# Moving expert weight splits between stages, and one subtraction between engines, in a four-layer kernel on one core

## Time and profile before

| | |
|---|---|
| median of three runs | 1728.53 us |
| profiled execution: time / span of the core | 1729.09 us / 1727.3 us |
| TensorE busy | 1576.4 us (91%) |
| VectorE busy | 1172.6 us (68%) |
| ScalarE busy | 931.7 us (54%) |
| GpSimd busy | 578.2 us (33%) |
| ternary layer | from about 652 to 907 us |
| features of the linear attention | from about 907 to 1094 us |
| its output and the routing | from about 1094 to 1206 us |

### The profile page before, as it was taken

One profiled execution on the slowest core, in us unless ns is written; L12 is line 12 of the kernel. 1 busy time (PEld: TensorE's weight loads), 2 busy tenths in 40 slices (PEclk: granted clock), 3 DMA queues, 4 the chain that ended last, 5 costly groups with the idle time before them and its releaser, 6 DMA issues. The chain is left out here.

```text
span 1727.3 us, 33567 instructions
## 1 busy us (share of the span) xinstructions
PE 1576.4 (91%) x12554; PEld 799.2 (46%) x12554; DVE 1172.6 (68%) x2074; ACT 931.7 (54%) x1641; POOL 578.2 (33%) x583
## 2 busy tenths in 40 slices
PE   5899999889999997999987999787898899999997
PEld 3533333354333343444433444454555566666564
DVE  4599998568999965899866777795623243333387
ACT  4756777445677765777645565476222333333332
POOL 4556565262000021222222121596271111111265
PEclk9999999999999999999998999899999999999999
DMA  6422331000000003666547999551151764456344
GB/s 232 140 55 56 69 75 38 13 2 2 14 2 2 2 2 77 137 143 137 105 91 267 320 330 336 198 180 68 63 94 50 279 234 167 154 186 220 99 125 135
DMA packets 177841, 211.42 MB, mean 122 GB/s; under 512 B 114202, under 2 KB 117624, under 8 KB 175504
## 3 DMA queue, kind: packets, MB, share of 16 engines
q1 hardware_dynamic: 170336, 188.54, 36.3%
q0 software_dynamic: 7344, 20.73, 4.5%
HBM read 193.33 MB, written 56.40 MB: 145 GB/s over the span
## 5 line engine op out<-in xcount | busy, mean ns | idle before, releaser
L751 ACT ACTIVATE layer_scratch<-banks 128x512 f32<-128x512 f32 x576 | 312.5, 595 | 129.5 <-PE banks L631 127.9
L862 DVE TENSOR_REDUCE layer_mx<-banks 128x2 f32<-128x1024 f32 (+3 forms) x304 | 339.2, 1155 | 24.1 <-PE banks L609 20.8
L2314 PE MATMUL banks<-wgate,sparse_xT 128*128 128x352 f16 x1128 | 184.4, 313 | 1.6 <-DVE sparse_xT L2392 1.6
L646 PE MATMUL banks<-layer_scratch,V 128*32 128x256 f32 x2304 | 174.5, 389 | 0.8 <-ACT layer_scratch L759 0.8
L2314 PEld LDWEIGHTS banks<-wgate,sparse_xT 128*128 128x128 f16 x1128 | 108.4, 98 | 62.1 <-DVE sparse_xT L2392 2.0
L1401 PE MATMUL banks<-arena,early 128*128 128x512 f16 x576 | 134.6, 384 | 0.3 <-DVE lin_relu L1561 0.3
L2398 DVE SCALAR_TENSOR_TENSOR sparse_hid<-sparse_th,banks 128x352 f32<-128x352 f32 x47 | 24.5, 521 | 154.0 <-ACT sparse_th L2359 154.0
L2425 POOL DMA_INDIRECT xg<-x_d,token x45 | 42.6, 947 | 249.2 <-PE banks L2304 249.2
L1840 PE MATMUL banks<-arena,xT 128*128 128x352 f16 x768 | 121.8, 315 | 2.0 <-PEq L2262 1.4
L1017 PE MATMUL banks<-wfcT,early 128*128 128x512 f16 x512 | 115.3, 383 | 7.3 <-ACT ffn_h L1159 6.5
L1145 PE MATMUL banks<-wprojT,ffn_hT 128*128 128x512 f16 x512 | 114.8, 383 | 7.3 <-DMA ffn_hT<-ffn_h 7.1
(11 more groups left out here) (300 smaller groups left out, 3033.4 us busy)
## 6 DMA issues: line engine op xcount, KB each, us to landing
wgate<-gate_d SPq DMA_DIRECT2D x47, 1408.0 KB
wdown<-down_d SPq DMA_DIRECT2D x47, 768.0 KB
lin_sp_raw<-in_L_ffn_w_gate_up_dram SPq DMA_DIRECT2D x52, 352.0 KB, 5.2
gate_d<-lin_sp_parts SPq DMA_DIRECT2D x52, 352.0 KB, 4.6
y_d<-y SPq DMA_DIRECT2D x47, 256.0 KB
down_d<-lin_sp_parts SPq DMA_DIRECT2D x39, 256.0 KB, 5.3
lin_sp_raw<-in_L_ffn_w_down_dram SPq DMA_DIRECT2D x26, 256.0 KB, 5.1
wfcT<-in_L_ffn_w_fc_dram SPq DMA_DIRECT2D x8, 512.0 KB, 8.2
```

Of the source, the lines that this page charges most:

```text
L646: last = pe.matmul(ps_o[32 * jj:32 * jj + 32, 256 * half:256 * half + 256], V[:, kt, 4 * jg + jj, :], prob[(2 * q + jj // 2) % 4][:, half, ...
L751: act.activation(prob[g % 4][:, par, :, :], ps_t[:, (2 * g + par) % 3, :, :], ACT.Exp, scale=HD ** -0.5).then_inc(exp_done, 1)
L862: dve.tensor_reduce(mx[x % 2][:, c, :, at:at + per], ps_s[:, 2 * (r % 2):2 * (r % 2) + 2, 0:per * n].rearrange("p e (h k) -> p e h k", k=n ...
L2314: last = pe.matmul(ps_g[u][n][rows, :], xT[u][:, a, k, rows], w, start=(k == 0 and i == 0), stop=(k == KC - 1 and i == 2), skip_group_chec ...
```

## The change

`FFN_EXPERTS` goes from 1 to 2 and `LIN_EXPERTS` from 14 to 15. The ternary layer splits 14 pieces in place of seven, one in each of 14 successive steps; the features stage still splits 13 experts (2 to 14 in place of 1 to 13); the output stage splits expert 15 and the half of the shared expert, 14 pieces in place of 21. In the output stage, `xlo` is the first function of VectorE's step instead of the first of GpSimd's.

```
-                unrolled(NT + AHEAD, [(0, of_layer(next_layer)), (3, xt), (3, split.every_second(split.load, sp)),
-                                      (5, of_layer(ht(0))), (5, of_layer(ht(1))), (7, split.every_second(split.store, sp))])
+                unrolled(NT + AHEAD, [(0, of_layer(next_layer)), (3, xt), (3, split.one_a_tile(split.load, sp)),
+                                      (5, of_layer(ht(0))), (5, of_layer(ht(1))), (6, split.one_a_tile(split.store, sp))])
...
-                                      (5, split.every_second(split.high, act))])
+                                      (4, split.one_a_tile(split.high, act))])
...
-                                      (1, of_layer(x_norm)), (1, of_layer(next_low)), (5, split.every_second(split.low, dve))])
+                                      (1, of_layer(x_norm)), (1, of_layer(next_low)), (4, split.one_a_tile(split.low, dve))])
...
-FFN_EXPERTS = 1
-LIN_EXPERTS = 14
+FFN_EXPERTS = 2
+LIN_EXPERTS = 15
...
-    def every_second(self, fn, eng):
+    def one_a_tile(self, fn, eng):
         def at(t):
-            if t % 2 == 0 and t // 2 < self.count:
-                fn(eng, t // 2)
+            if t < self.count:
+                fn(eng, t)
         return at
...
+                def xlo(t):
+                    u = t % 2
+                    dve.wait_ge(xh_done, t + 1)
+                    after(dve, xt_done, t - 1)
+                    after(dve, stored[u], 16 * (t // 2))
+                    dve.tensor_tensor(x2[u][:, 1, :], m.X[:, t, :], x2[u][:, 0, :], ALU.subtract).then_inc(xl_done, 1)
...
-                unrolled(NT, [(5, residual), (1, gating), (0, stats), (9, levac),
+                unrolled(NT, [(7, xlo), (5, residual), (1, gating), (0, stats), (9, levac),
                               (2, split.spread(split.low, dve, NT)), (4, router)])
...
-                unrolled(NT, [(7, xlo), (2, wlo), (5, root_r), (1, product), (0, lambda t: ln_q.root(pool, t, t % 2))])
+                unrolled(NT, [(2, wlo), (5, root_r), (1, product), (0, lambda t: ln_q.root(pool, t, t % 2))])
```

More of the change, by code:

```diff
@@ L1814, in wlo @@
                     pool.tensor_tensor(w2[u][:, 1, :], w[u][:, :], w2[u][:, 0, :], ALU.subtract).then_inc(wl_done, 1)
[L1816 to L1821, removed]
                 def root_r(t):
```

## The result

The changed kernel takes 1731.72 us in the median of 20 runs (1728.64 to 1742.21), the kernel before 1725.78 in 20 runs of the same set (1720.45 to 1731.77). The ratio is 1.0034, with a 95% interval from 1.0022 to 1.0046: 5.9 us slower (3.8 to 7.9). The two intervals share 3.8 to 4.8 us. The forecast was 1.4 us slower, with a range of 1724 to 1736.

The account below looks back on a forecast made before the run. The prediction took the ScalarE, VectorE and GpSimd round to bound the ternary layer and VectorE the changed output stage. Terms +5.4 - 2.2 - 0.7 - 0.6 - 0.5 = +1.4 us gave 1730 us, range 1726 to 1733, 8 in 10 within 1724 to 1736.

Parts of the forecast that it names:

- Which chain sets the ternary layer: Ternary layer: the round of ScalarE, VectorE and GpSimd, at 14.1 or 13.96 us mean, sets the pace over TensorE's 13.82.
- Rival C: Ternary layer: added pieces are hidden under TensorE and cost 0, giving 1725 us; chance 0.10.
- The price of the pieces, +5.4: Ternary layer: seven added pieces lengthen the round, four at 0.89 and three at 0.61 us, 5.4 us in all.
- 14.3 or 14.55 us apart in all of tiles 1 to 12: Ternary layer: expected trace sign, the spacing of h_clip starts once every step holds a piece.
- DMAs at 0: Ternary layer: seven more loads and seven more stores on SyncE's queue cost 0, up to 1 us if landings lengthen.
- Features at 0: Features stage: 13 experts split before and after in the same 91 piece shapes and order, so no change in time.
- The output stage, -4.0: Output stage: middle nine steps -2.2 us, start -0.7 and -0.6, end -0.5.
- the check (51.7): Output stage middle: second estimate for nine steps, built from one measured step of 5.13 us, giving 51.7 us.
- the -0.7 and -0.6: Output stage start: step 2 loses its piece and most of a wait, -0.7 us; step 5 loses one of two pieces, -0.6.
- Rival A: Output stage: xlo on VectorE waits up to 1.12 us a step for GpSimd's wlo, giving 1741 or 1735 us; chance 0.16.
- Rival B: Output stage: GpSimd alone is the bound, so the middle gives -8.4 us, total 1723 to 1724; chance 0.12.
- The +3.6: Whole kernel: the forecast change in us if the output stage's middle gives 0 in place of -2.2.

Follow-up runs that it names:

- a5_hidden7: The kernel before with only its seven ternary pieces moved into gaps of the round, xlo on GpSimd; 1721.04 us, ratio 0.9958.
- a6_output_only: The kernel before with the changed kernel's output stage; expert 1 unsplit, its table rows filled with copies of expert 0 by seven further stores; 1723.82 us, ratio 0.9974.
- a3_hidden: The changed kernel with its 14 ternary pieces moved into gaps of the round on ScalarE and VectorE; 1717.02 us, ratio 0.9944 to before.
- a8_after: The changed kernel unaltered, timed again in a second set of runs; 1729.76 us, ratio 1.0012 to before.
- a2_xlo_only: The kernel before with only xlo moved to VectorE, 7 ternary and 21 output pieces kept; 1734.02 us, ratio 1.0037.
- a1_splits_only: The changed kernel with xlo back on GpSimd, so only the pieces are moved; 1730.52 us, ratio 1.0018 to before.

## Why the prediction was right, point by point

*Which chain sets the ternary layer.* Right, and it was the step that mattered: TensorE was 99.8% busy there and not the bound. Rival C is out: the pieces were not hidden under TensorE, while `a5_hidden7` shows that the place in the round was what they cost.

*The price of the pieces, +5.4.* Right. I had put all seven added pieces into the round; six are there, for 4.4 us, and the seventh stands ahead of the first `h_clip`, for 0.88, together 5.3. My sign "14.3 or 14.55 us apart in all of tiles 1 to 12" was wrong for the steps at both ends, which are shorter with and without a piece. The layer as a whole: 265.1, 265.8 and 264.2 us with seven pieces, 272.0, 270.1 and 269.5 with 14; the means differ by 5.5. What I had not counted is inside that: the `proj` behind the wait took 8.75, 9.51 and 8.37 us with seven pieces, 9.92, 9.18 and 8.75 with 14, 0.4 us more in the mean.

*DMAs at 0.* Right (`a6_output_only`: seven further stores, round unchanged; `a3_hidden`: 14 loads and stores, round 4.8 us shorter than before).

*Features at 0.* 177.2, 176.5 and 175.9 us with seven pieces ahead of it, 177.6, 176.8 and 177.6 with 14: 0.8 us in the means, which executions that differ by 4.0 us over all ten profiles do not tell from nothing.

*The output stage, -4.0.* This is the term that was mis-sized: it measured -2.3 (112.5 and 113.2 us against 110.1 to 110.8; against the 112.5 alone, -1.7 to -2.4). The mechanism was right: VectorE's sum is the bound once `xlo` is there, 5.74 to 5.94 us a step. The middle came out at 51.85 us, by the check (51.7) and not by the sum (50.8) or the mean that I took (51.2), so -1.5 in place of -2.2. The sum had a 704-wide piece at 0.71 us from start to start, read from one that waited; with nothing beside it, it takes 0.81 (679.28 to 680.09 above). At the start I took the -0.7 and -0.6 (measured: -0.71 up to the first residual, -0.59 in the next step) and forgot that the step after it, ahead of 1122.62, holds the first `xlo` and a 704-wide piece in place of a 512-wide one: it grew from 5.13 to 5.94 us. At the end the residuals closed up by 0.9 us, and then the stretch behind the last of them took 13.2 to 13.9 us in all six profiles with `xlo` on VectorE, against 12.7 in all four with `xlo` on GpSimd. My -0.5 for the end was about +0.1. In five of the six (13.7 to 13.9) it is TensorE's clock, which was low in the first block of the shared expert, 12 matmuls of 128x352. Here is this block in `a8_after`, and then before, with the granted clock in the first column behind the busy time:

```profile
1193.40:1197.20 3.80, 3.80 (x30) 0.55 0.18 69
```

```profile
1196.60:1198.60 2.00, 2.00 (x24) 1.00 0.00 0
```

Twelve matmuls that take 1.95 us took 3.55, and 3.40 to 3.61 in the five. The same wait of 1.38 or 1.39 us for ScalarE stands ahead of the block in all ten profiles, and in the first profile of the changed kernel the clock stayed full behind it; why it falls in the others is open. The 0.5 us that this profile has over before come by another way. GpSimd's root stands beside the moved `xlo` and takes 1.07 us, where it took 0.55, and TensorE waits 0.81 us for the evacuation by ScalarE that hangs on it, where it waited 0.29. First the changed kernel (VectorE, GpSimd, TensorE), then before (GpSimd, TensorE):

```profile
1198.63 0.68 DVE L1796 TENSOR_TENSOR out_x<-X,out_x 128x512 f16<-128x512 f32 x1
1198.65 1.07 POOL L1826 TENSOR_TENSOR out_lnr_rstd<-out_lnr_var,minus_half 128x1 f32<-128x1 f32 x1 [2.53 <-DVE out_lnr_var L221]
1202.62 0.61 PE L170 MATMUL banks<-ident,out_x 128*128 128x128 f16 x8 [0.81 <-ACT xT L1755]
```

```profile
1195.78 0.55 POOL L1827 TENSOR_TENSOR out_lnr_rstd<-out_lnr_var,minus_half 128x1 f32<-128x1 f32 x1 [2.23 <-DVE out_lnr_var L221]
1199.23 0.61 PE L170 MATMUL banks<-ident,out_x 128*128 128x128 f16 x8 [0.29 <-ACT xT L1756]
```

*Rival A.* Not in the changed kernel, by the reason given (VectorE comes 0.4 us ahead), except in one step. `a2_xlo_only` shows the point from which it decides: the second piece in a step.

*Rival B.* Out. The steps stayed above 5.7 us with GpSimd idle for a quarter of the time. And in `a1_splits_only` the same nine steps take 52.1 us with `xlo` on GpSimd, against 51.85 with it on VectorE (a step with one 704-wide piece 5.96 against 5.94). With 14 pieces the two placements of `xlo` cannot be told apart; with 21 pieces the move costs 5.5 us. The Trainium skill ("Perfetto Trace Analysis", "Optimizing Scalar/DVE Operations") warns that such a move "might not help"; these runs agree. The +3.6 that I had worked out from this warning lies near the measured sum, but by luck: it had the middle unchanged, and the middle shortened by 1.5 us, since five of its 13 pieces left it.

*The sum.* With the terms as measured, +5.5 + 0.8 - 2.3 = +4.0 us, where the two sets agree (3.8 to 4.8). The forecast said 1.4, and its range held. That the time itself, 1731.72 us, lies only 1.7 from the forecast 1730 is in part luck: the kernel before came out at 1725.78 us in this set, 2.75 below the 1728.53 that I had built on. (The bounds of my two stages give 1726.8 to 1734.2, not the 1726 to 1733 that I wrote; the measured time lies in both.) The first set alone lies just above the border that I had set between no change and slower; I had given 0.20 to that side.

## What to carry to other kernels

An engine that is 99.8% busy is not the bound if the chain beside it has the longer period: read the period of each from start to start of the same instruction, in steps with and without the added work, and multiply. Small work that fills no gap is paid in full even on an engine with 10% idle; the same work moved to where each engine already waits for the other added nothing to the stage (here 12 us between the two places in the ternary layer, 9 of them in the round). Before moving an operation between VectorE and GpSimd, sum VectorE's step first: a gap-free GpSimd may be waiting for VectorE inside its instructions (the root L226 shows 1.20 us beside VectorE's piece, one with no long VectorE instruction beside it 0.55).

## What the runs showed of the hardware

Waits of 3.6 to 4.7 us ahead of the 32 matmuls (128x512) of `proj` of tile 14 were followed by 8.4 to 9.9 us for them in all seven profiles that have such a wait, against 7.07 at the full level of 2.4 GHz; in the changed kernel the granted clock over that stretch was 0.70, so part of it ran at the 1.2 GHz level. Behind waits of 0.9 us or less they took 7.07. At the start of the layer, too, a wait of 3.3 to 3.5 us was followed by a `proj` of 8.8 to 10.0 us (the kernels with 14 pieces that are not all hidden). Waits of 2.5 to 2.7 us there were followed by either: 7.08 in three profiles (before, `a2_xlo_only`, `a3_hidden`), 8.4 to 8.8 in the three others. And behind the 1.38 or 1.39 us ahead of the shared expert the clock was low in five profiles and full in five. So the length of the wait alone does not say which it will be. The wait at tile 14 costs 1.3 to 2.9 us more than itself in every profile that has it, and removing it in `a3_hidden` gave that back, which my expectation for that run had left out.
